# Edge loop of a four-layer graph kernel: a limit of 500 bytes on the descriptors of three groups of transfers

## The reference, cut to what matters

```python
score = s_src + s_dst + einsum(diff, a_dif) + einsum(abs(diff), a_abs) + einsum(hr_src * hr_dst, a_prd)
alpha = leaky_relu(score, 0.2)
ex    = exp(alpha_t - segment_max(alpha_t, src)[src])
att   = ex / segment_sum(ex, src)[src]
out   = segment_sum(att * h_e[dst], src)          # diff = hr[dst] - hr[src], per edge
```

## Time and profile before

| | us |
|---|---|
| median of 3 runs | 2567.65 |
| profiled execution | 2566.56 |
| its span | 2564.8 |
| PE busy | 2226.7 (87%) |
| DVE busy | 1095.5 (43%) |
| ACT busy | 728.3 (28%) |
| POOL busy | 539.8 (21%) |

### The profile page before, as it was taken

The page is one execution under the profiler, slowest core; times in us unless marked ns, Lnnn a source line. Parts: engine busy times, 40 slices in busy tenths (PEclk is TensorE's granted clock), DMA queues, the critical chain, the costliest instruction groups (busy, mean ns, idle before and its releaser), DMA issues.

```text
span 2564.8 us, 22909 instructions
## 1 busy us (share of the span) xinstructions
PE 2226.7 (87%) x7917; PEld 1258.5 (49%) x7917; DVE 1095.5 (43%) x2478; ACT 728.3 (28%) x1206; POOL 539.8 (21%) x474
## 2 busy tenths in 40 slices
PE   6798864888999798879798898899798889999998
PEld 3476543676445453334454454455345454444443
DVE  8786662896323323344453354335325430000002
ACT  1475542775321110002151142124115011111111
POOL 4676642443210100010101101100110120012201
PEclk9899886897999789988899899899899989999999
DMA  9432234221021100022102101200301057777742
GB/s 376 109 59 43 42 80 99 63 56 50 1 86 66 50 0 19 1 85 90 49 1 61 59 0 47 72 0 0 115 10 43 15 211 298 300 288 299 296 189 64
DMA packets 61468, 243.14 MB, mean 95 GB/s; under 512 B 23183, under 2 KB 25699, under 8 KB 39244
## 3 DMA queue, kind: packets, MB, share of 16 engines
q1 hardware_dynamic: 31866, 174.12, 19.2%
q0 software_dynamic: 26336, 62.19, 8.0%
q10 hardware_dynamic: 3168, 5.63, 0.6%
HBM read 209.96 MB, written 31.92 MB: 94 GB/s over the span
## 4 chain that ended last, share of the span: by engine, by line
PE 55%; DVE 16%; issue 13%; DMA 7%; ACT 4%; POOL 3%; PEldq 0%; PEld 0%; SPq 0%; DVEq 0%; POOLq 0%; ACTq 0%
PE PS L724 18%; PE PS L731 10%; PE PS L1221 6%; PE PS L1230 6%; PE PS L1259 6%; DMA pair_scores<-TS,SIDX 5%; DVE ST L1893 1%; PE PS L1020 1%; POOL pair_scores L1754 1%; DVE Y L1901 1%; DVE AR L2184 1%; PE PS L1239 1%; PE PS L769 1%; DVE Y L2454 1%; DVE Y L2455 1%
## 5 line engine op out<-in xcount | busy, mean ns | idle before, releaser
L724 PE MATMUL PS<-XT,WR 128*128 128x113 f32 (+2 forms) x1264 | 363.6, 448 | 9.6 <-ACT XT L1327 7.6
L1725 POOL TENSOR_TENSOR RSTD<-VE,HALF 125x1 f32<-125x1 f32 x105 | 73.6, 701 | 1144.0 <-DVE VE L1896 1144.0
L724 PEld LDWEIGHTS PS<-XT,WR 128*128 128x128 f32 (+1 forms) x1264 | 199.7, 196 | 182.2 <-issue 180.1
L870 PE MATMUL PS<-HR,HOT 125*125 125x512 f32 x800 | 219.0, 423 | 47.5 <-DVE HOT L2041 47.5
L731 PE MATMUL PS<-WR,XT 128*125 128x512 f32 (+1 forms) x480 | 214.6, 601 | 6.6 <-ACT XT L1653 4.3
L2628 DVE TENSOR_TENSOR AR<-AR,PS 128x512 f32<-128x512 f32 (+1 forms) x44 | 30.3, 688 | 404.0 <-PE PS L1230 404.0
L724 PE MATMUL PS<-AR 125*128 125x512 f32 (+3 forms) x680 | 193.5, 439 | 9.3 <-ACT AR L1625 3.9
L870 PEld LDWEIGHTS PS<-HR,HOT 125*125 125x125 f32 x800 | 152.1, 198 | 91.3 <-DVE HOT L2041 40.6
L1918 DVE TENSOR_TENSOR AR<-PS,AR 125x512 f32<-125x512 f32 x55 | 38.1, 692 | 311.5 <-PE PS L731 311.0
L731 PE MATMUL PS<-WR,AR 128*125 128x512 f32 (+1 forms) x370 | 157.2, 576 | 10.3 <-ACT AR L1658 4.6
L724 PEld LDWEIGHTS PS<-AR 125*128 125x128 f32 (+1 forms) x680 | 106.1, 189 | 98.0 <-issue 89.1
(11 more groups left out here) (392 smaller groups left out, 3669.5 us busy)
## 6 DMA issues: line engine op xcount, KB each, us to landing
WR<-in_qkv SPq DMA_DIRECT2D x12, 1024.0 KB
WR<-in_omm SPq DMA_DIRECT2D x12, 1024.0 KB
pair_scores<-CNT SPq DMA_DIRECT2D x1, 12212.0 KB, 56.0
AR<-pair_scores SPq DMA_DIRECT2D x5, 2187.5 KB
AR<-in_x_a SPq DMA_DIRECT2D x10, 1024.0 KB, 9.7
AR<-in_x_b SPq DMA_DIRECT2D x10, 1024.0 KB, 4.8
AR<-in_x_c SPq DMA_DIRECT2D x10, 1024.0 KB, 7.0
WR<-in_x_a SPq DMA_DIRECT2D x8, 1024.0 KB, 8.9
```

The source lines that it names most:

```text
L724: last = mm(s.ap[0:parts, c0:c1], lhs(k), rhs(k)[:, c0:c1], start=(k == 0), stop=(k == terms - 1))
L870: last = mm(DIFF[m % 4], HOT[g % 2][0:P, k, tile(j)], HR[0:P, k, :, b, :], start=(k == 0 and b == 0), stop=(k == NT - 1 and b == 1))
L1725: g.tensor_tensor(RSTD[:, t:t + 1], VE[:, t:t + 1], HALF[:, :], ALU.pow)\
```

## The change

Three calls that issue transfers get the argument `max_dma_last_dim=ROW_BYTES`, with `ROW_BYTES = 500`. It cuts the last dimension of a transfer, which is the run of bytes that one descriptor moves, into pieces of at most 500 bytes. What is moved, the issuing engine, the queue, the order, the buffers and the semaphores stay as they are. The transfers are the ids of a chunk (`edge_ids`, 10 times two), the edge attributes of a group (`edge_rows`, 20 times two) and the pair sums (5 times four).

```diff
+ROW_BYTES = 500
             def edge_ids(j):
                 for r, name in enumerate(("src_p", "dst_p")):
                     ids = a[name].rearrange("p e -> (p e)")
-                    sp.dma_start(IDB[j % 2][:, r, :], bcast(ids, 1000 * j, 1000, 128))\
-                      .then_inc(ids_in[j % 2], 16)
+                    sp.dma_start(IDB[j % 2][:, r, :], bcast(ids, 1000 * j, 1000, 128),
+                                 max_dma_last_dim=ROW_BYTES).then_inc(ids_in[j % 2], 16)
 
             def edge_rows(g):
                 for lo, hi in zip(WIDE_ROWS, WIDE_ROWS[1:]):
                     sp.dma_start(ER[g % 4][lo:hi].rearrange("p a b -> p (a b)"),
-                                 a["edge_attr"][lo:hi, 256 * g:256 * (g + 1)]).then_inc(edge_in[g % 4], 16)
+                                 a["edge_attr"][lo:hi, 256 * g:256 * (g + 1)],
+                                 max_dma_last_dim=ROW_BYTES).then_inc(edge_in[g % 4], 16)
...
                         sp.dma_start(SUMS_IN[b][lo:hi].rearrange("p q c -> p (q c)"),
                                      pair_sums[b][N * (P * t + lo):N * (P * t + hi), :].rearrange(
-                                         "(p q) c -> p (q c)", q=N)).then_inc(sums_in, 16)
+                                         "(p q) c -> p (q c)", q=N),
+                                 max_dma_last_dim=ROW_BYTES).then_inc(sums_in, 16)
```

## The result

| | us |
|---|---|
| before, 13 runs beside the changed kernel | 2568.75 median (2561.18 to 2574.45) |
| changed, 13 runs | 2573.18 median (2566.8 to 2579.64) |
| ratio of the changed to the one before | 1.0024, 95% interval 1.0013 to 1.0034 |
| profiled execution of the changed kernel | 2569.18, its span 2567.4 |

2536 us was forecast, a gain of 32 us, with a range of 2521 to 2569 us. There is a loss of 0.24%, some 6 us (the interval: 0.13 to 0.34%), and the median lies 4 us above the range. The loss is just above the 0.2% that this kernel's measurement can tell from no change.

The account below looks back on a forecast made before the run. From 117.66 us on, POOL's list and the landing of puts were taken to bound the loop. Terms of -20, -14, +0.3 and +0.7 us gave -33, rounded to -32: forecast 2536 us, range 2521 to 2569 us.

Parts of the forecast that it names:

- The long turns: POOL's loop of puts: 13 turns, eight beside ids and five beside pair sums, exceed the others by together 44 us.
- rival 4: Loop: another bound comes up at once, PE at 11.5 us a group or the start; no change, 2567 us; chance 0.08.
- The limit works in bytes: Argument of the three load calls: it counts bytes, so a chunk of ids has 2,048 data packets in place of 256.
- rival 3: Load calls: the limit counts elements, ids go in 2,000-byte pieces, attributes stay whole; gain 26 us, 2541 us; chance 0.07.
- A descriptor of 500 bytes costs 0.035 us: DMA engines: price of one small descriptor, taken between 0.024 and 0.041 us; a 4,000-byte packet costs 0.146 us.
- What an indirect transfer waits for is a count of descriptors.: Puts and adds beside loads: each waits for some 16 descriptors whatever their size, 0.55 us at 500 bytes.
- even turns: DMA engines: packets are taken from two queues one and one, whatever their size; nine of some 16 waited for.
- Ids -20, pair sums -14 us: Long turns of POOL: gain 20 us at the eight chunks of ids and 14 us at the five pair-sum loads.
- Edge attributes 0, start +0.7, first rows +0.3 us: Attribute loads count zero (bounds -5 and +5 us); later clears cost 0.7 us, the very first attribute rows 0.3 us.
- Rival 1: Long turns: a put waits for bytes or the whole transfer, each wait growing 1.4 to 1.5 us; 2587 us; chance 0.14.
- step at 64: Puts beside loads: a bundle of up to 64 descriptors goes ahead, 2.2 us a wait; gain 17 us, 2550 us; chance 0.11.

Follow-up runs that it names:

- experiment 1: Kernel before, without most ids of chunks 2 to 9 and most pair sums of tiles 1 to 4: 2540.62 us beside 2571.43, ratio 0.9881.
- experiment 4: Kernel before, with the clear of the pair table in 22,016 descriptors of 568 bytes in place of 1,024 of 12,212: 2599.57 us beside 2571.43.
- experiment 6: Kernel before, with only ids and edge attributes in 500-byte descriptors, pair sums whole: 2571.94 us beside 2568.15, ratio 1.0015.
- experiment 2: Kernel before, with descriptor limits of 4000 to 100 bytes for ids and 5000 to 200 for pair sums, varied by chunk and tile: 2569.96 us.
- experiment 8: Kernel before, with ids, edge attributes and pair sums in thirds, each issued right after a put has landed: 2555.33 us, ratio 0.9947.
- experiments 9 and 10: Kernel before, ids transfers of chunks 2 to 9 cut to fewer rows, ids or both, in two orders of sizes: 2545.32 and 2546.13 us beside 2566.73.

## Why the prediction was wrong, step by step

- *The long turns are 44 us and lie on the path; nothing else bounds the loop.* Right: experiment 1 made the kernel 31 us shorter, its last put started 30.3 us earlier, and rival 4 falls.
- *The limit works in bytes.* Right; rival 3 falls. The last chunk shows 578 + 424 + 443 = 1,445 packets by 313 us and not 512 in all, and 0.29 MB / 578 = 500 bytes each.
- *A descriptor of 500 bytes costs 0.035 us.* Right within its bounds of 0.024 and 0.041: at the ids, while q1 is alone, 16 x 2 x 0.539 / 578 = 0.030 us, and 16 x 0.730 / 443 = 0.026 us later; at the pair sums 16 x 5 x 1.114 / 2197 = 0.041 us. At the lowest price the 128 of an engine would be through in 3.4 us; they take 5.0 us (309.8 to 314.7 us), since the engines stay at 70%.
- *"What an indirect transfer waits for is a count of descriptors."* This is the step that failed. It was drawn from two equal counts, 16 and 17, at 12,212 and 8,192 bytes, two sizes only a factor of 1.5 apart, and from the assumption that 9 of the 16 were even turns. With a third point a factor of 20 away (experiment 4) the count is some 140. With 500-byte ids, 78 to 130 per engine go ahead of a put's last packet, with pair sums 155 to 160. The count of 16 to 19 at the puts of the kernel before was no second witness: a load of ids has 18 packets per engine there and a load of pair sums 19, so it was the whole load. The even turns of the earlier trace rows, 103 and 102 packets, are real there, but they aren't what delays a put beside ids: at 309 to 311 us one queue passes 36 descriptors per engine and the other none.
- *Ids -20, pair sums -14 us.* Measured +0 and +3 us. Both terms hang on the failed step alone.
- *Edge attributes 0, start +0.7, first rows +0.3 us.* The first put starts 0.9 us earlier than before in the profile, and the longer of the turns with attributes take 4.2 to 4.4 us where they took 4.0 to 4.2: within the bounds. SP did stand longer at one issue, 15.80 us in place of 1.55, as the row shows:

```profile
12.87 15.80 SPq L533 DMA_DIRECT2D AR<-in_dst_p  x1
```

  It issued the clears from 36.11 us on in place of 15.84, yet SP's later loads were through at about the same time (69.8 us in place of 68.4), and nothing of that came onto the path.
- *Rival 1, a wait for bytes or for the whole transfer, 0.14.* This is what happened, as a wait for the whole load under way. The prediction set it aside for the equal counts beside the clear; the packets' times in the trace of before would have spoken for it. Its price was wrong: it let each load, and with it each wait, grow by 1.4 to 1.5 us. From first to last packet a load of ids grew from 4.4 to 5.5 us in the mean of eight, and a load of pair sums from 5.7 to 6.4 us. The waits grew less, by 0 and 0.6 us: in five of the eight chunks of ids the put no longer comes at the load's end but 0.5 to 2.2 us before it, since 500-byte pieces that are issued with it or after it do not all go ahead.
- *Where the 0.24% is.* The traces do not locate it. The five turns at the pair sums are 3 us longer, but other turns make up for it: in the two profiled executions the loop, first put to last, takes 308.2 us (changed) and 307.9 us (before), and the last put starts 0.6 us earlier in the changed kernel. Its span is 2.6 us longer all the same: behind the last put, where nothing was changed, it takes 3.2 us more; single executions of one kernel differ by more than that. What experiment 6 costs is measured as a sum and not located either.

**What stays open.** The wait ends, in most long turns, when the load that was issued before the put has been moved; rows, bytes and phase all act through when that is. That rests on the packets' times of the kernel before, the changed one and experiments 1, 2 and 8. Which stage of the DMA path makes the put wait was not shown: the trace has when a packet is moved, not when its descriptor lies ready. Nor is it shown what lets an add or a put go ahead of the end of a load with very many descriptors, after some 140 of them per engine in experiment 4 and 150 to 160 at 200 and 100 bytes. The page of the Trainium skill named above, section "Queues, rings and completion order", has an engine change between queues after a packet of 9 to 17 descriptors, at most 64. The even turns at 52 us agree with a change after each descriptor. Beside the put of 354.05 us, 1,939 packets of the load, 121 per engine, are moved between 355.6 us, when that put is due, and 360 us, while 30 of its own 32 come, all after 359 us; that is more than 64, and experiment 2 shows no step at 64.

## What to carry to other kernels

When a small indirect transfer is late behind a bulk load, cutting the load's descriptors does not let it through. Look in the trace for when the last packets of both come: if they come together, what counts is when the load ends. Issue loads one at a time, each at the moment at which such a transfer has just landed (13 us, 0.5%, for the ids), and make them shorter in time; fewer bytes in as many rows did that (experiment 8), and so did fewer rows (experiments 9 and 10). A mechanism that is read off two operating points should be held to a third one far away before a sum is built on it: here two sizes 1.5 apart gave the same count, and a factor of 20 would have shown it false. Split a load over several turns only where each turn has slack of its own; without it the wait is divided and its sum stays.

## What the runs showed of the hardware

- A put's last packet comes with the last packet of the load issued before it, within 0.15 us in 10 of 13 long turns of the kernel before, with 18 or 19 packets per engine, and in 7 of 13 of the changed one, with 130 or 160.
- Rows of 32 bytes come at some 110 per us over all 16 engines, with these 5% busy (experiment 1), while pieces of 500 bytes of longer rows come at 443 per us. In this kernel a short row takes as long as several pieces of a long one.
- Small pieces into DRAM are dearer than small pieces out of it. With the engines full, an engine passes a piece of 568 bytes written in 0.059 us (experiment 4) and one of 500 bytes read in 16 x 5 / 2,197 = 0.036 us (354 to 359 us in the changed kernel).
- An issue behind a long list of descriptors stands: 15.8 us behind the first ids in 500-byte pieces, where it stood 1.55 us behind whole rows, and three issues 100.9 us behind the clear of 568-byte ones. That it stands for room in the queue is inferred.
